# Mixture-of-experts on one core: down products of a short last tile in two column groups, and the next expert's first step in both arms of its branch

## The reference

```python
x = x + attention(layernorm(x), ctx)          # 4 batches x 1024 rows x 1024
h = layernorm(x).reshape(4096, 1024)
top4, idx = top_k(h @ gate_w.T + gate_b, 4)   # 32 experts, softmax weight of 4
for every expert e, on the rows sent to it:
    gate = min(rows @ w_gate[e] + b_gate[e], 7)             # 1024 -> 512
    up   = clip(rows @ w_up[e] + b_up[e], -7, 7)
    act  = (up + 1) * gate * sigmoid(1.702 * gate)
    outs = act @ w_down[e] + b_down[e]                      # 512 -> 1024
x = x + sum over the 4 experts of weight * outs
```

## Time and profile before

| | us |
|---|---|
| median of 3 runs | 3029.32 |
| lowest, highest | 3028.07, 3030.02 |
| the profiled execution | 3032.38 |
| its span, first to last instruction | 3030.6 |
| mean granted TensorE clock (share of full) | 0.986 |
| TensorE busy in the span | 97% |
| VectorE, ScalarE, GpSimd busy | 56%, 39%, 19% |

### The profile page before, as it was taken

The page is one execution under the profiler, slowest core; times in us unless marked ns, Lnnn a source line. Parts: engine busy times, 40 slices in busy tenths (PEclk is TensorE's granted clock), DMA queues, the critical chain, the costliest instruction groups (busy, mean ns, idle before and its releaser), DMA issues.

```text
span 3030.6 us, 44774 instructions
## 1 busy us (share of the span) xinstructions
PE 2927.8 (97%) x14948; PEld 1507.3 (50%) x14949; DVE 1702.7 (56%) x2536; ACT 1191.3 (39%) x1221; POOL 564.5 (19%) x502
## 2 busy tenths in 40 slices
PE   6899999959999999999999999999999999999997
PEld 3455555535544444554554545445544554455453
DVE  5787887644535555555554555655555654553532
ACT  3343333223423434444343444434444443442421
POOL 1132333321111111111111111111111111111111
PEclk8999999979999999999999999999999999999999
DMA  7977766654645555666654656675655555564433
GB/s 218 221 209 181 181 178 167 193 173 137 196 127 166 158 161 154 173 184 196 194 143 129 206 164 176 193 213 161 166 164 157 170 161 158 168 186 125 83 63 63
DMA packets 343540, 501.37 MB, mean 165 GB/s; under 512 B 190881, under 2 KB 190881, under 8 KB 343234
## 3 DMA queue, kind: packets, MB, share of 16 engines
q0 software_dynamic: 45856, 152.33, 22.9%
q10 hardware_dynamic: 94576, 225.46, 21.2%
q1 hardware_dynamic: 203058, 122.94, 15.9%
HBM read 354.64 MB, written 112.46 MB: 154 GB/s over the span
## 4 chain that ended last, share of the span: by engine, by line
PE 77%; DMA 0%; ACTq 0%; issue 0%; ACT 0%; POOL 0%; DVE 0%; SPq 0%; POOLq 0%
PE psY L1327 24%; PE psG L1305 22%; PE psU L1305 22%; PE psX L1311 4%; PE psG L1363 3%; PE psA L1318 2%; DMA acc<-y,idxs 0%; DMA idxs<-slots 0%; ACTq L1064 0%; ACT xT L1166 0%; ACTq L1092 0%; POOL acc L1157 0%; PE psU L1364 0%; DVE y L1246 0%; ACT y L1177 0%
## 5 line engine op out<-in xcount | busy, mean ns | idle before, releaser
L1327 PE MATMUL psY<-W,aT 128*128 128x512 f16 x3456 | 769.5, 379 | 1.4 <-ACT aT L1170 1.4
L1305 PE MATMUL psG<-W,xT 128*128 128x512 f16 x3072 | 686.2, 380 | 6.9 <-ACT xT L1166 5.6
L1305 PE MATMUL psU<-W,xT 128*128 128x512 f16 x3072 | 684.0, 379 | 0.0
L1327 PEld LDWEIGHTS psY<-W,aT 128*128 128x128 f16 x3456 | 337.4, 98 | 377.6 <-ACT aT L1170 1.7
L1305 PEld LDWEIGHTS psG<-W,xT 128*128 128x128 f16 x3072 | 299.4, 98 | 373.9 <-issue 14.0
L1305 PEld LDWEIGHTS psU<-W,xT 128*128 128x128 f16 x3072 | 300.1, 98 | 334.4
L1133 POOL DMA_INDIRECT acc<-y,idxs x143 | 225.6, 1578 | 1056.2 <-DVE y L1246 1012.6
L1246 DVE SCALAR_TENSOR_TENSOR y<-bias,idxs,y 128x1024 f32<-128x1024 f32 x143 | 183.7, 1284 | 395.2 <-ACT y L1177 395.2
L676 PE MATMUL psM<-W,XT 128*128 128x512 f16 x1392 | 358.7, 382 | 5.7 <-DVE xr L936 5.7
L1166 ACT ACTIVATE xT<-psX 128x1024 f32<-128x1024 f32 x145 | 148.1, 1022 | 477.6 <-PE psX L1311 451.4
L1177 ACT ACTIVATE y<-psY,idxs 128x1024 f32<-128x1024 f32 x143 | 159.3, 1114 | 444.1 <-DMA idxs<-slots 440.9
(11 more groups left out here) (168 smaller groups left out, 2595.8 us busy)
## 6 DMA issues: line engine op xcount, KB each, us to landing
stage_more<-in_L_ffn_w_down ACTq DMA_DIRECT2D x62, 1024.0 KB, 9.6
stage<-in_L_ffn_w_gate ACTq DMA_DIRECT2D x60, 1024.0 KB, 7.0
stage_more<-in_L_ffn_w_up ACTq DMA_DIRECT2D x31, 1024.0 KB, 5.6
stage<-in_L_ffn_w_up ACTq DMA_DIRECT2D x30, 1024.0 KB, 12.5
stage<-in_x SPq DMA_DIRECT2D x32, 512.0 KB, 5.6
xr<-in_x SPq DMA_DIRECT2D x32, 512.0 KB, 4.9
acc<-xr SPq DMA_DIRECT2D x32, 512.0 KB, 3.8
xn_tab<-x2h SPq DMA_DIRECT2D x32, 512.0 KB, 3.0
```

Of the source, the lines that this page charges most:

```text
L1305: op = pe.matmul(ps[:], xT[:, k, :, a], weights(par, c, offset + k * I, I), start=k == 0 and n == 0, stop=k == KH - 1 and n == 2)
L1327: op = pe.matmul(psY[:, h * HALF:(h + 1) * HALF], aT[:, k, :, a], weights(par, c, 2 * KH * I + k * H + h * HALF, HALF), start=k == 0 and n ...
```

## The change

Down products of a half tile, and the 4 transposes of its activations, take `rows=64`. The 24 down matmuls are then issued in pairs: columns 0 to 511 of the output go to partitions 0 to 63 of `psY`, columns 512 to 1023 to partitions 64 to 127. Since the down products stand in the next expert's first step, that step is written twice, once in each arm of the branch on the half tile, on TensorE and VectorE. The first step of the first expert stands ahead of the loop over pairs, which has one turn less; the last two experts stand behind it. The three register loads of an expert now stand behind its first step, not ahead of it. Result: ScalarE now makes `y = weight * bias`, without a wait for the down products; VectorE then does `y = psY * weight + y`, in two operations of 64 rows for a half tile. Down products wait for this VectorE operation of the tile before (`s_y`).

```diff
@@ ScalarE
-            def weigh_y(i):
+            def weigh_bias(i, par):
 
                 act.wait_ge(s_idxs, 16 * i + 16)
                 act.wait_ge(s_added, i + 1)
-                act.wait_ge(s_Y, i + 2)
-                act.activation(y[:], psY[:], ACT.Copy, scale=idxs[:, 2:3].bitcast(F32)).then_inc(s_y0, 1)
+                act.activation(y[:], bias[:, par, 2 * I:], ACT.Copy, scale=idxs[:, 1:2].bitcast(F32)).then_inc(s_y0, 1)
...
@@ VectorE
-            def finish_y(i, par):
-
-                dve.wait_ge(s_y0, i + 2)
-                dve.scalar_tensor_tensor(out=y[:], in0=bias[:, par, 2 * I:], scalar=idxs[:, 1:2].bitcast(F32), in1=y[:],
-                                         op0=ALU.mult, op1=ALU.add).then_inc(s_y, 1)
...
+            def finish_y(i, tile_y, tile_idx, rows=P):
+
+                dve.wait_ge(s_y0, i + 1)
+                dve.wait_ge(s_Y, i + 2)
+                weight = tile_idx[0:rows, 2:3].bitcast(F32)
+                if rows == P:
+                    dve.scalar_tensor_tensor(out=tile_y[:], in0=psY[:], scalar=weight, in1=tile_y[:],
+                                             op0=ALU.mult, op1=ALU.add).then_inc(s_y, 1)
+                    return
+                dve.scalar_tensor_tensor(out=tile_y[0:rows, 0:HALF], in0=psY[0:rows, 0:HALF], scalar=weight,
+                                         in1=tile_y[0:rows, 0:HALF], op0=ALU.mult, op1=ALU.add)
+                dve.scalar_tensor_tensor(out=tile_y[0:rows, HALF:], in0=psY[P - rows:P, HALF:], scalar=weight,
+                                         in1=tile_y[0:rows, HALF:], op0=ALU.mult, op1=ALU.add).then_inc(s_y, 1)
...
@@ TensorE
                 for n in range(KI):
-                    op = pe.transpose(psA[:, n * P:(n + 1) * P], ahl_w[:, n * P:(n + 1) * P], ident[:])
+                    op = pe.transpose(psA[:, n * P:n * P + rows], ahl_w[0:rows, n * P:(n + 1) * P], ident[0:rows, 0:rows])
                 op.then_inc(s_A, 1)
 
-            def down(i, par):
+            def down(i, par, rows=P):
+
                 pe.wait_ge(s_aTev, i + 1)
-                pe.wait_ge(s_y0, i + 1)
-                for h in range(2):
+                pe.wait_ge(s_y, i + 1)
+
+                def product(h, k, n):
+                    a, c = PASSES[n]
+                    at_row = 0 if rows == P or h == 0 else P - rows
+                    return pe.matmul(psY[at_row:at_row + rows, h * HALF:(h + 1) * HALF], aT[:, k, 0:rows, a],
+                                     weights(par, c, 2 * KH * I + k * H + h * HALF, HALF),
+                                     start=k == 0 and n == 0, stop=k == KI - 1 and n == 2)
...
+            def expert(e, par, last=False):
+
+                t0, tf, t1 = start_of(pe, e), full_end_of(pe, e), start_of(pe, e + 1)
+
+                def then(rows):
+                    if not last:
+                        step(t1, e + 1, 1 - par, True, rows)
+                    else:
+                        transpose_act(t1 - 1, rows)
+                        down(t1 - 1, par, rows)
+
+                with pe.Fori(t0 + 1, tf) as i:
+                    step(i, e, par, False)
+                with pe.If(t1 > tf):
+                    half_step(tf, par)
+                    then(P // 2)
+                with pe.Else():
+                    then(P)
```

More of the change, by code:

```diff
@@ L1277, in step @@
                                          op0=ALU.mult, op1=ALU.subtract).then_inc(s_alo, 1)
[L1278 to L1282, removed]
-                for par in range(2):
[L1284 to L1295, removed]
+                if split:
+                    cut_lo(dve, e + 1, 1 - par, CUT[j][2])
+                if follows:
+                    finish_y(i - 1, y, idxs, rows_before)
+            def expert(e, par, splits, next_splits):
+                t0, tf, t1 = start_of(dve, e), full_end_of(dve, e), start_of(dve, e + 1)
+                def then(rows):
+                    if next_splits is not None:
+                        step(t1, e + 1, 1 - par, 0, next_splits, rows_before=rows)
+                    else:
+                        finish_y(t1 - 1, y_last, idxs_last, rows)
+                for j in range(1, len(CUT)):
+                    step(t0 + j, e, par, j, splits)
+                with dve.Fori(t0 + len(CUT), tf) as i:
+                    step(i, e, par, None, False)
+                with dve.If(t1 > tf):
+                    step(tf, e, par, None, False, rows=P // 2)
+                    then(P // 2)
+                with dve.Else():
+                    then(P)
@@ L1297, in _ @@
+            dve.sem_inc(s_y, 1)
+            step(0, 0, 0, 0, True, follows=False)
+            with dve.Fori(0, PAIRS - 1) as pair:
+                for par in range(2):
+                    expert(pair * 2 + par, par, True, True)
+            expert(E - 2, 0, True, False)
+            expert(E - 1, 1, False, None)
         @block.tensor
@@ L1349, in step @@
                 transpose_rows()
-                guarded(pe, prev_guard, lambda: down(i - 1, 1 - par if first else par))
-                weights_cut(3 * PER_W)
+                if follows:
+                    down(i - 1, 1 - par if first else par, rows_before)
+                weights_split(3 * PER_W)
             def half_step(i, par):
@@ L1373, in _ @@
             transpose_rows()
-            with pe.Fori(0, PAIRS) as pair:
+            step(0, 0, 0, True, follows=False)
+            with pe.Fori(0, PAIRS - 1) as pair:
                 for par in range(2):
-                    e = pair * 2 + par
-                    t0, tf, t1 = start_of(pe, e), full_end_of(pe, e), start_of(pe, e + 1)
-                    step(t0, e, par, True, pair > 0 if par == 0 else None)
-                    with pe.Fori(t0 + 1, tf) as i:
-                        step(i, e, par, False, None)
-                    with pe.If(t1 > tf):
-                        half_step(tf, par)
-            tt = start_of(pe, E)
-            transpose_act(tt - 1)
-            down(tt - 1, 1)
+                    expert(pair * 2 + par, par)
+            expert(E - 2, 0)
+            expert(E - 1, 1, last=True)
 _INS = ["x", "ctx_1024", "L0_xattn_Wq", "L0_xattn_bq", "L0_xattn_Wk", "L0_xattn_bk", "L0_ffn_gate_w", "L0_ffn_gate_b",
```

63 lines of the change are left out of this document (36 added, 27 removed).

## The result

The changed kernel takes 3004.57 us (median of 4 runs, 3001.28 to 3005.97) against 3028.7 us for the kernel before (4 runs, 3026.34 to 3030.02): a ratio of 0.9916, 95% interval 0.9904 to 0.9929. It is 24 us faster; 3015 was forecast, with 2988 to 3024 as the range.

A forecast was written before the change was run, and what follows sets the result against it. TensorE's stream was taken to bound the kernel. Short down products -41.4, entering the form +1.6, transposes 0, holes +21.6 and +6.3, old holes -2.2 and -0.2 gave -14.3 us: 3015 us, range 2988 to 3024.

The forecast's parts named there:

- rival A: At expert ends: TensorE's sequencer reaches the branches early enough that no hole opens; -39.3 us, 2990 us, chance 0.17.
- Rival D: Paired down matmuls do not overlap because both write psY; nothing gained, 3027 to 3031 us, chance 0.02.
- the control work at an expert's end: Branches and loads behind short down products open holes: 2.4 us at nine loop ends, 0.9 at seven others.
- The cover: Queued down products hide control work at expert ends; the short group shrinks this by 2.59 less 0.10 us.
- The slack: Reserve at loop ends: taken as none, since full-tile loop ends already show a hole of 0.04 us.
- the old surplus: Six half-tile loop ends exceed 5.18 us, laid to control work after TensorE's release by `aT`; 2.2 us in sum goes.
- The estimate from the queue's depth: TensorE's queue of 64 instructions covers 6.05 us before and 3.5 to 3.6 after, giving a hole of 2.5 us.
- Into the short form: Cost of entering paired form before a half tile's down products: 0.10 us each, 1.6 us on for 16.
- Transposes of 64 rows: Four activation transposes per half tile: between -3.5 and +4.5 us for 16, taken as 0.
- the new wait: Down products wait for VectorE's `y` of the tile before: costs nothing; without margin, 0.5 to 1 us in few half steps.
- B: Control at half-tile expert ends takes longer, holes 0.9 us longer each; sum 0, 3029 us, chance 0.11.
- C: The longer loop over pairs refetches code, 3.69 us at each of 15 turns; +41 us, 3070 us, chance 0.06.

The follow-up runs named there:

- with long down products: Changed kernel with the half tiles' down products and transposes of h back in full width, rest of the change kept: 3025.97 us, ratio 0.9989.
- the case with early loads: Changed kernel with the next expert's three register values loaded ahead of the branch on the half tile and carried in registers: 2990.88 us, ratio 0.9875.

## Why the prediction was right where it was, and where it was not

**Direction and range** held, the range with some luck: 3004.57 us lies just below the 3006 to 3024 that the forecast gave itself, and inside 2988 to 3024 because that takes in rival A. That holes open was right; they were put at nearly twice their size. The gain held too: in the short groups 24 matmuls run in 2.59 us, 41.4 us in sum. Rival D (pairs do not overlap) is out.

**The holes were mis-sized.** The step that failed is the one on the control work at an expert's end. Forecast were 2.4 us nine times and 0.9 seven times, 27.9 in sum; measured 10.4 and 4.4, together 14.8. Two parts of it:

- *The cover.* I bounded the handing over of 48 instructions by 2.6 us, took the rest of the time since `aT`'s release as control work, at least 5.7 us, and concluded that the whole down group belongs to the cover, which would shrink by 2.49. The sequencer's records say otherwise: control at an expert's end is at most 3.85 us long in the kernel before where its loads are undisturbed, and it starts at a fixed 1.32 us behind the long and 0.27 us behind the short group. The cover falls from 3.86 to 2.32, by 1.54. The release of `aT` has no part in it: after the change the down products start 1.4 to 5.5 us behind it, and the holes are the same.
- *The slack.* I took the 0.04 us of the full-tile loop ends for all loop ends. But control is 3.84 us there and 3.36 at an undisturbed half-tile loop end (at 2058.97 it ended 0.50 us ahead of the gate product). In the changed kernel it is 3.44. So 0.04 + 1.54 - 0.40 = 1.18 us is what the hole had to be, against 1.17 measured.

**The cause of the old surplus was wrong, its size right.** I put it on a late release. In the kernel before, L1082 at the worst end (same columns as above) reads

```profile
L1082 PEldq TENSOR_LOAD <-tile_start x2: 303/864/1426, 1393.3 to 1396.0; - x2
```

The first load took 1.43 us instead of 0.30, and that is the hole. The six ends with a surplus have a first load of 0.86 to 1.43 us; at ends inside a pass 0.89 to 1.26 occur as well, but there the slack covers them. The surplus is gone in the kernel after, with long down products (control now stands a step later) and with early loads. What slows such a load stays open. Work of VectorE and GpSimd lies beside the slow ones, but a load at 2060.8 took 0.31 us beside much the same work. The late release goes with such loads, but does not make a hole by itself. All nine half-tile ends of the kernel before with such a load had `aT` ready 2.3 to 3.5 us ahead of the down products, the seven others 4.5 us or more; but three of the nine, inside a pass, show no hole, so that the forecast's line between 3.5 and 4.5 us held for loop ends alone. In the kernel after, where the loads stand a step later, releases 1.4 and 1.9 us ahead go with loads of 0.30 us.

**The estimate from the queue's depth** agreed with my wrong bound and so lent it weight. By the Trainium skill (TensorE: Matmul & The Clock Gate, table at the head) the queue holds 64 instructions. In the trace 3.86 us at 5.18 / 24 us for a matmul and its weight load is 18 pairs, 36 instructions, still to run when control starts; behind the short group 2.32 us at 2.59 / 24 is 21.5 pairs, 43. No record shows the depth of the queue itself. The measurement decides: the cover is worth 36 to 43 instructions here.

**Smaller terms.** Into the short form: the down products start 0.97 us behind psX instead of 0.87, 0.10 as forecast. Transposes of 64 rows: forecast 0 within -3.5 to +4.5, measured 16 x 0.06 = +1.0. The old 0.04 at full-tile ends went, as forecast. Nothing was charged for the new wait: right in the steps but for one wait of about 0.1 us. At the end, where I had not looked for the cover, the last down products do wait for VectorE, 1.6 us more than before, which costs nothing while the clock stays full. That the end hangs on the indices, and gains nothing from the new way of y, was right.

The sum with measured terms: -41.4 + 14.8 + 1.6 + 1.0 - 2.2 - 0.2 = -26.4, beside -26.8 in the trace up to the last row transposes. With the 1.6 of the last wait it is -24.8, beside -25.2 up to the last down products.

**The rivals.** A (no hole) is out for the changed kernel; the case with early loads is what it described, and 2990 is what it gave. B (holes 0.9 us longer each) is out. Control did not get shorter at half-tile ends, though: at a loop end it went from 3.36 to 3.44 us (undisturbed loads), and inside a pass, where I had it shorter by at least 0.84 than at a loop end, from 2.40 to 2.95, 0.49 less than at a loop end. The holes stayed under the forecast because a half-tile end used less of the cover than I took it to, and less of the cover went. C (code fetched again) is out. The queue of instructions in the kernel after:

```profile
q8 instruction: 33, 0.54, 0.1%
```

That is 33 packets against 27. Between 900 and 2830 us there is no packet in this queue; 4 fall between 2830 and 3000, where the last pair, now written out behind the loop, runs for the first time. A second instruction queue, q14, has one packet after 900 us, at 2819 us, also there, and none after 900 us in the kernel before; the 27 packets of the forecast are those of q8 alone. The loop of eight steps stays where it is, as that of six did. By the two-page rule of the Trainium skill (Runtime: NRT & Kernel Launch, Instruction fetch mechanics) the longer loop, too, would fetch at every turn; the trace of the kernel after disagrees, as that of the kernel before did.

## What to carry to other kernels

Shortening the work in front of a branch or a loop end also shortens what hides it. Read the sequencer's own records there: when its first control instruction starts, how long it runs and when the next product starts give the hole that a shorter group will leave, and no bound by other events can replace that. If a hole would open, move register loads to where a long group is still queued; that was worth 14 us here, behind short groups, and 1 us in the kernel before, behind long ones.

## What the runs showed of the hardware

- A bounded value loaded into a register costs TensorE's sequencer 0.75 us (0.64 without a new index): load 0.30, register operation 0.15, test 0.02, the rest gaps. A branch taken at the loop's end is 0.22, the jump over the other arm 0.17.
- Such a load can take 0.86 to 1.43 us (nine half-tile ends of the kernel before); the cause is open.
- The sequencer came to control work at a fixed place in the group, 1.32 us behind the start of a long one and 0.27 behind that of a short one. Worked out from the rest of the group, it was 36 to 43 instructions ahead of the array.
- Holes of 2.7 to 3.0 us between experts lowered the granted clock to 0.91 or 0.92 over the following step in four of eight cases, for 1.5 to 1.7 us each; holes up to 2.0 us did not. Idle times of 2.5 to 3.2 us ahead of the last down products did so in two of seven profiles. With 1.68 us behind it, a hole of 2.73 us costs 1.6 times its own length.
